# Two PSUM banks for B's broadcast and two, not three, for the ring of TensorE results

## The chip, the cores and the metric

The kernel runs on one core of one Trainium2 chip. The metric is the time of one execution on the device, in microseconds. It was run three times: the median is 8001.87 us, the lowest 7986.92, the highest 8004.43. Engines are called TensorE (PE in the profile, PEld its weight loads), VectorE (DVE), ScalarE (ACT), GpSimd (POOL) and SyncE (SP, which issues the DMAs).

## The reference

The input is 16 samples of 64 x 64 positions (tokens) with 96 channels. Two layers follow each other, each of them `x = x + layer(groupnorm(x))`, in 32 groups of three channels.

```python
# layer 0: a pointwise block between band-limited resamplings
xu = upsample_rfft(gn(x))                 # 64x64 -> 128x128
h  = xu @ W1.T + b1                       # 96 -> 384
h  = c0 + c1 * h + c2 * h * h
h  = h @ W2.T + b2                        # 384 -> 96
x  = x + lowpass_rfft(h)[::2, ::2]
# layer 1: Mamba over the 4096 tokens of a sample
xs, z = split(gn(x) @ W_in.T)             # 192 channels each
xc = silu(conv3(xs) + conv_b)
dt, B, C = split(xc @ W_x.T)              # 6, 16, 16
delta = softplus(dt @ W_dt.T + b_dt)
h_t = exp(delta_t * A) * h_{t-1} + delta_t * B_t * xc_t    # 192 x 16 states
y_t = sum_n(h_t * C_t) + xc_t * D
x  = x + (y * silu(z)) @ W_out.T
```

## The kernel before, in words

Each engine has one list of instructions, written out in the program's order, and semaphores between them. Layer 1 of sample s is what the loop runs on. The other work, of the samples behind it, is threaded in between: the S steps (transposes and the first half of the upsampling) of sample s + 2, the W steps (second half, W1, square, W2, first half of the low pass) and the D steps (second half of the low pass, residual) of sample s + 1.

A sample has 8 chunks (`NC8`) of 512 tokens. A chunk has 24 units (`NU`), and a unit is one scan: 32 channels x 4 states on 128 partitions, 512 tokens. Three units make a group, so there are 8 groups (`NG`) a chunk. For each group

- TensorE broadcasts the rows of B to 128 partitions in PSUM: `spread_b`, one bf16 matmul with `selb` into `pb` (L744),
- VectorE multiplies it with `rep_u` for three units at once into `b3`, in PSUM (L1021),
- VectorE does three scans `hs <- av, b3` (L1027), each of which needs its exponential `av` from ScalarE (L882; there are 8 buffers, so ScalarE can be 8 units ahead),
- GpSimd multiplies each with C into `hc` (L1068), and
- TensorE sums them over the states into `py` (`reduce`, L755; L752 adds the skip term at each half chunk). VectorE gates `py` (L1035), once at unit 15 and once at unit 3 of the chunk behind.

In TensorE's list the `spread_b` of group g + 1 stands at unit 3g + 1, and the `reduce` of group g at unit 3g + 5. `spread_b` waits until VectorE has done the product that read `pb` last, that of group g.

All other results of TensorE go through `cb`, a ring of PSUM banks, in steps: a step is one name in a plan (`plan_of`), and step i writes bank i modulo `RING`. It has to wait until the step that had the bank before was read (`freed_all([i - RING] + ...)`, L619). Most steps are read ("evicted") by ScalarE (L825, L832, L841, L856, L861, L867, L872), OUT at L800; SG, DG, WG and PAD by VectorE. The names are:

- W_up (two matmuls of L663, read at L825), W_f (L669, read with a square at L832), W_2 (twelve of L674, L825), W_dn (L680, L825),
- ST (L634), SA and SB (L639), D_lo and D_hi (L692 and L696; they wait for their loads `rr`, which SyncE issues as steps finish),
- the batch of a chunk, which stands in units 8 to 11 of TensorE's list: X, X (L708), Z, Z (L714), DBC (L718), DT, DT (L723) for the chunk two ahead,
- OUT (L735 and L736) at unit 6, and PAD (L622), which does nothing but bring a plan to a multiple of `RING`.

A plan has rows; a row is the unit at which a step stands in TensorE's list. W steps are spread evenly over the free rows of a sample (none stands in units 8 to 11 of a chunk). The other engines do their part of a step some units later in their own lists: `LAG` is 6 for ScalarE, 3 for VectorE, 2 for GpSimd, 1 for SyncE. The batch is evicted by ScalarE in one go at unit 14, with a table load ahead of the first silu, one ahead of the softplus, and one ahead of the next exponential, that of unit 15.

A full sample's plan has 273 steps. Ahead of the first sample lie 291 more with no scans beside them. The last sample has only batches and OUT.

Of the kernel before, what the change touches and what calls it, by code (L numbers as in the profile page):

```python
# [9 lines left out]
ALU = mybir.AluOpType  # L10
ACT = mybir.ActivationFunctionType

NS, HH, WW, C = 16, 64, 64, 96
# [8 lines left out]
T = 512  # L22
NC8 = L // T
NJ, NQ = DI // 32, DSTATE // 4
NU = NJ * NQ
NG = NU // 3
NHC, NAV, NHS = 6, 8, 6
XB_H = 8
LEAD = 2
RING = 3  # L30

# [20 lines left out]
def w_steps():  # L54
    out = []
    for b in range(NB + 3):
        if b < NB:
            out += [("W_up", b, r) for r in range(2)]
        if 1 <= b <= NB:
            out += [("W_f", b - 1, f) for f in range(NF)]  # L60
        if b >= 3 and (b % 2 == 0 or b == NB + 2):
            out.append(("W_dn", (b - 3) // 2))
        if 2 <= b <= NB + 1:
            out.append(("W_2", b - 2))
    return out
# [35 lines left out]
def padded(rows):  # L101
    rows = sorted(rows, key=lambda r: r[0])
    n = sum(st[0] not in UNRINGED for _, st in rows)
    return rows + [(rows[-1][0], ("PAD", i)) for i in range(-n % RING)]

# [30 lines left out]
def build(nc, A):  # L136
    ctx = ExitStack()
    with ctx:
        def sb(name, shape, dt=F32):
            return ctx.enter_context(nc.sbuf_tensor(name, shape, dt))  # L140

        def ps(name, shape):
            return ctx.enter_context(nc.psum_tensor(name, shape, F32))

        def sem(name):
            return ctx.enter_context(nc.semaphore(name))
# [15 lines left out]
        ident = sb("ident", [128, 128])  # L162
# [19 lines left out]
        selb = sb("selb", [C, NQ, 128], BF16)  # L182
# [17 lines left out]
        dm = sb("dm", [C, 2])  # L200
        spare = sb("spare", [C, RING])
        vv = sb("vv", [C, 2])
# [18 lines left out]
        bc3 = sb("bc3", [C, 4, T], BF16)  # L221
# [15 lines left out]

        cb = ps("cb", [128, RING, 512])
        b3 = ps("b3", [128, 3, 512])
        pb = ps("pb", [128, 512])  # L240
        py = ps("py", [128, 512])

        ld_w = sem("ld_w")
# [4 lines left out]
        pe_conv = sem("pe_conv")  # L248
        cb_free = [sem(f"cb_free{i}") for i in range(RING)]
        xb_ld = [sem("xb_ld0"), sem("xb_ld1")]  # L250
# [28 lines left out]
        pe_b = sem("pe_b")  # L279
        act_a = sem("act_a")  # L280
        dve_bu = sem("dve_bu")
# [35 lines left out]
        N_FREE = len(loads) - 2  # L317

        HEAD = w_steps()[:W_HEAD] + [("WLD", 0), ("WG", 0)]
        SETUP_STEPS = 3  # L320
        N_SETUP = 14
        BEFORE = [alone([("SLD", 0)] + s_steps() + [("SG1", 0), ("SG2", 0)]),
                  alone([("WLD", 0), ("WG", 0)] + w_steps(), [("SLD", 0)] + s_steps()),
# [4 lines left out]
        def ringed(plan):  # L328
            return sum(st[0] not in UNRINGED for _, st in plan)

        UF = ringed(FULL)
        starts = [SETUP_STEPS]
        for plan in BEFORE:
            starts.append(starts[-1] + ringed(plan))
        base_full = starts[-1]
        base_tail = base_full + LOOPS * UF
        assert ringed(FIRST) == UF and UF % RING == 0 and all(v % RING == 0 for v in starts)

        class Steps:
# [22 lines left out]
            def freed(self, i):  # L362
                return count(cb_free[i % RING], self.thirds + (i // RING + 1))

# [34 lines left out]
        def count(sm, v):  # L399

            return max(v, 0)
# [194 lines left out]
        def _(pe):  # L596
# [5 lines left out]
            for f in range(NF):  # L602
                mm = pe.matmul(cb[0:C, 1, 0:1], w2t[:, f, :], fcst[:, f:f + 1], start=(f == 0), stop=(f == NF - 1))
            mm.then_inc(pe_conv, 1)
            pe.transpose(cb[0:C, 2, 0:C], ident[0:C, 0:C], ident[0:C, 0:C]).then_inc(pe_conv, 1)
            pe.wait_ge(setup_v, count(setup_v, N_SETUP))
            pe.wait_ge(setup_a, count(setup_a, 2))

# [130 lines left out]
            def spread_b(G, k, g):  # L739

                if g == 0:
                    pe.wait_ge(pool_bc, count(pool_bc, G * 2 + 2))
                pe.wait_ge(dve_bu, count(dve_bu, G * NG + g))
                pe.matmul(pb[:, :], selb[:, g % NQ, :], bc3[:, k % 4, :], start=True, stop=True).then_inc(pe_b, 1)  # L744

            def reduce(s, k, g):
                G = s * NC8 + k
                hf, q = g // NQ, g % NQ
                pe.wait_ge(pool_hc, count(pool_hc, G * NU + 3 * g + 3))
                if q == 0:  # L750
                    pe.wait_ge(dve_y, count(dve_y, G * 2 + hf))
                    pe.matmul(py[0:C, :], ddiag[:, hf, :], xcs[:, k % 4, hf, :], start=True, stop=False,  # L752
                              skip_group_check=True)
                for j in range(3):
                    mm = pe.matmul(py[32 * j:32 * j + 32, :], rsel[:, :], hc[:, (3 * g + j) % NHC, :],  # L755
                                   start=False, stop=(q == NQ - 1), skip_group_check=True)
                mm.then_inc(pe_red, 1)

            def unit(s, k, n):
                G = s * NC8 + k  # L760
                if G == 0 and n == 0:
                    spread_b(G, k, 0)
                if n % 3 == AT["pe"]["pb"]:
                    if n // 3 + 1 < NG:
                        spread_b(G, k, n // 3 + 1)
                    elif not (G + 1 == NS * NC8):
                        spread_b(G + 1, k + 1, 0)
                if n % 3 == AT["pe"]["red"] % 3 and n >= AT["pe"]["red"]:
                    reduce(s, k, (n - AT["pe"]["red"]) // 3)

# [145 lines left out]
        def _(dve):  # L916
# [24 lines left out]
                setup(dve.tensor_scalar(ddiag[:, t, :], ident[0:C, 0:C], dskip[:, t:t + 1], None, ALU.mult))  # L941
            dve.wait_ge(setup_a, count(setup_a, 2))
            setup(dve.tensor_scalar(nega[:, :, :], nega[:, :, :], -1.0, None, ALU.mult))
            dve.wait_ge(pe_conv, count(pe_conv, 3))
            dve.tensor_copy(wlin[:, :], cb[0:C, 0, 0:C]).then_inc(cb_free[0], 1)
            dve.tensor_tensor(cbase[:, :], cb[0:C, 1, 0:1], b2t[:, :], ALU.add).then_inc(cb_free[1], 1)
            dve.tensor_copy(spare[:, 2:3], cb[0:C, 2, 0:1]).then_inc(cb_free[2], 1)
            assert n_set[0] == N_SETUP

            def step(st, key):  # L950
# [61 lines left out]
            def unit(s, k, n):  # L1012
                G = s * NC8 + k
                hf, g, q = n // 12, n // 3, n // 3 % NQ
                if n == 0:
                    dve.wait_ge(ru_ld[k % 2], count(ru_ld[k % 2], s * (4 * 64) + (k // 2 + 1) * 64))
                if n % 3 == 0:

                    dve.wait_ge(pe_b, count(pe_b, G * NG + g + 1))
                    dve.wait_ge(dve_h, count(dve_h, G * NU + n))  # L1020
                    dve.tensor_tensor(b3[:, :, :], rep_u[:, k % 2, 3 * hf:3 * hf + 3, :],  # L1021
                                      pb[:, None, :].broadcast_to([128, 3, T]), ALU.mult).then_inc(dve_bu, 1)
                    dve.wait_ge(pool_st, count(pool_st, G * NG + g + 1 - NHS // 3))
                    dve.wait_ge(dve_bu, count(dve_bu, G * NG + g + 1))
                dve.wait_ge(act_a, count(act_a, G * NU + n + 1))
                start = state[:, g, n % 3:n % 3 + 1] if k > 0 else zero_state[:, 0:1]
                dve.tensor_tensor_scan(hs[:, n % NHS, :], av[:, n % NAV, :], b3[:, n % 3, :], start, ALU.mult, ALU.add)\  # L1027
                    .then_inc(dve_h, 1)
                if n == AT["dve"]["y0"]:
                    gate(G, k, 0)  # L1030
# [141 lines left out]
```

## Time and profile before

| | |
|---|---|
| median of three runs | 8001.87 us |
| profiled execution | 7987.5 us |
| its span | 7985.7 us |
| granted TensorE clock, mean | 0.857 |
| TensorE busy | 6793.7 us, 85% |
| VectorE busy | 5981.0 us, 75% |
| ScalarE busy | 4697.4 us, 59% |
| GpSimd busy | 4578.7 us, 57% |
| L1021 `b`, x1024 | 1803.6 us busy, 1761 ns each |
| L1027 scans, x2688 and x384 | 3279.1 and 466.8 us busy, 1264 ns each |
| L744 broadcast, x1024 | 439.8 us busy, 429 ns each |

Busy is the time in which an engine ran an instruction, as a share of the span. The clock is the granted share of 2.4 GHz: 1.00 is the upper level and 0.50 the lower one, 1.2 GHz. An idle time is put down to the instruction that released the engine. In the rows below, a window's line has its start and end, its length, then each engine's busy time with the number of instructions, then the clock and the DMA engines' share and rate.

### The profile page before, as it was taken

The page shows a single profiled execution, that of the slowest core. Times are in us where ns is not written, and L with a number is a line of the kernel's source. Part 1 is how long each engine was busy: PE and PEld are TensorE (multiplying, and loading weights), DVE is VectorE, ACT ScalarE, POOL GpSimd, SP SyncE. Part 2 cuts the span into 40 slices and gives each one's busy share as a digit, 9 for nine tenths or more (in the row PEclk, how much of TensorE's full clock was granted, in tenths as well). Part 3 has the DMA queues.
Part 4 walks back from the last instruction along what each step waited for, and adds up shares of the span by engine and source line. Part 5 has one row for each costly group of instructions (what it writes and reads, how often), then busy time and mean ns, then how long its engine had stood idle before and what let it go on. Part 6 is the DMA issues. An engine that isn't in the chain of part 4 may idle for free. (4 is left out here: it accounts for less than half of the span.)

```text
span 7985.7 us, 102095 instructions
## 1 busy us (share of the span) xinstructions
PE 6793.7 (85%) x33686; PEld 3470.3 (43%) x33686; DVE 5981.0 (75%) x4943; ACT 4697.4 (59%) x8260; POOL 4578.7 (57%) x4516
## 2 busy tenths in 40 slices
PE   7897988979898897988979888897988979888666
PEld 5543444434344443444434444444443534444212
DVE  0287868778786886868778687787878878687788
ACT  4464756657475564756647566564755647566454
POOL 0265646656565564656656466565656656466566
PEclk8797988979798897988979889797998979889666
DMA  3455555545555554555555545555555655554542
GB/s 84 111 130 127 128 130 116 135 119 131 133 125 127 117 135 121 131 133 118 127 127 131 132 111 137 119 131 132 124 132 114 144 122 130 125 127 115 122 112 66
DMA packets 805834, 983.44 MB, mean 123 GB/s; under 512 B 391258, under 2 KB 417542, under 8 KB 805318
## 3 DMA queue, kind: packets, MB, share of 16 engines
q1 hardware_dynamic: 805318, 976.92, 51.8%
q8 instruction: 280, 4.59, 0.3%
q14 instruction: 236, 1.93, 0.1%
HBM read 717.71 MB, written 259.00 MB: 122 GB/s over the span
## 5 line engine op out<-in xcount | busy, mean ns | idle before, releaser
L1068 POOL TENSOR_TENSOR hc<-hs,cs 128x512 f32<-128x512 f32 x3072 | 3843.2, 1270 | 3022.5 <-DVE hs L1027 2005.9
L1027 DVE TENSOR_TENSOR_SCAN hs<-av,state,b 128x512 f32<-128x512 f32 x2688 | 3279.1, 1264 | 171.7 <-ACT av L882 97.2
L1021 DVE TENSOR_TENSOR b<-rep_u,pb 128x1536 f32<-128x1536 f32 x1024 | 1803.6, 1761 | 1215.3 <-PE pb L744 1152.7
L882 ACT ACTIVATE av<-rep_d,nega 128x512 f32<-128x512 f32 x3072 | 2124.8, 714 | 303.5 <-DVE hs L1027 299.6
L755 PE MATMUL py<-hc,rsel 128*32 128x512 f32 x6144 | 1292.4, 711 | 37.4 <-POOL hc L1068 36.6
L669 PE MATMUL cb<-xu,w1a 96*128 96x392 f32 x2400 | 1030.0, 540 | 86.3 <-ACT t1s L825 40.4
L674 PEld LDWEIGHTS cb<-w2c,g 128*98 128x98 f32 x9600 | 945.3, 177 | 193.2 <-issue 125.0
L674 PE MATMUL cb<-w2c,g 128*98 128x96 f32 x9600 | 973.2, 261 | 7.6 <-ACT g L832 6.6
L832 ACT ACTIVATE g<-cb,b1a 128x392 f32<-128x392 f32 x1200 | 686.3, 583 | 230.5 <-PE cb L669 215.2
L744 PE MATMUL pb<-bc,selb 96*128 96x512 bf16 x1024 | 439.8, 429 | 319.3 <-DVE b L1021 319.3
L708 PE MATMUL cb<-xn,wtap 96*96 96x512 f32 x1536 | 705.5, 609 | 1.1 <-ACT xn L904 1.1
L669 PEld LDWEIGHTS cb<-xu,w1a 96*128 96x128 f32 x2400 | 424.1, 198 | 558.6 <-issue 284.6
L841 ACT ACTIVATE x1s<-cb,cst 96x256 f32<-96x256 f32 x256 | 118.7, 470 | 644.4 <-PE cb L696 434.7
L663 PE MATMUL cb<-up_h,t1r 64*96 64x98 f32 x3200 | 386.1, 275 | 115.6 <-DVE b1a L999 60.4
L1027 DVE TENSOR_TENSOR_SCAN hs<-av,zero_state,b 128x512 f32<-128x512 f32 x384 | 466.8, 1264 | 14.3 <-ACT av L882 2.8
L692 PE MATMUL cb<-xt,wtot 96*96 96x256 f32 x512 | 240.8, 566 | 254.2 <-DMA rr<-v_scratch 158.0
L708 PEld LDWEIGHTS cb<-xn,wtap 96*96 96x96 f32 x1536 | 244.5, 166 | 475.2 <-issue 474.3
L755 PEld LDWEIGHTS py<-hc,rsel 128*32 128x32 f32 x6144 | 165.3, 115 | 633.3 <-issue 439.6
L663 PEld LDWEIGHTS cb<-up_h,t1r 64*96 64x96 f32 x3200 | 283.7, 169 | 350.2 <-issue 197.4
L825 ACT ACTIVATE vr<-cb 98x384 f32<-98x384 f32 x400 | 195.0, 488 | 407.5 <-PE cb L674 407.5
L856 ACT ACTIVATE xcs<-cb,tapb 96x512 f32<-96x512 f32 x256 | 175.0, 683 | 428.0 <-PE cb L708 428.0
L752 PE MATMUL py<-xcs,ddiag 96*96 96x512 f32 x512 | 328.4, 728 | 92.8 <-DVE xcs L1035 92.8
(102 smaller groups left out, 6762.8 us busy)
## 6 DMA issues: line engine op xcount, KB each, us to landing
rep_d<-delta_scratch SPq DMA_DIRECT2D x512, 384.0 KB, 7.2
rep_u<-deltax_scratch SPq DMA_DIRECT2D x512, 384.0 KB, 9.4
cs<-c_scratch SPq DMA_DIRECT2D x512, 256.0 KB, 5.6
delta_scratch<-dlt SPq DMA_DIRECT2D x128, 384.0 KB, 3.1
deltax_scratch<-dlt SPq DMA_DIRECT2D x128, 384.0 KB, 4.0
t_scratch<-t1s SPq DMA_DIRECT2D x128, 300.0 KB
t1r<-t_scratch SPq DMA_DIRECT2D x160, 240.0 KB, 5.0
rr<-v_scratch SPq DMA_DIRECT2D x256, 150.0 KB
```

The lines of the kernel that those rows point to most:

```text
L663: mm = pe.matmul(bank[0:C, e * GH:(e + 1) * GH], t1r[half, m % 2, i2 % 5, :], up_h[half, GH * r:GH * r + GH], start=True, stop=True)
L669: mm = pe.matmul(bank[:, 0:BC], w1a[:, 128 * f:128 * f + 128], xu[:, b % 2, :], start=True, stop=True)
L674: mm = pe.matmul(bank[0:GH, C * j:C * j + C], g2[:, b % 2, f, GH * j:GH * j + GH], w2c[:, f, :], start=(f == 0), stop=(f == NF - 1))
L708: mm = pe.matmul(bank[0:C, :], wtap[:, tap, t, :], xn[:, k2 % 2, tap:tap + T], start=(tap == 0), stop=(tap == 2))
L744: pe.matmul(pb[:, :], selb[:, g % NQ, :], bc3[:, k % 4, :], start=True, stop=True).then_inc(pe_b, 1)
L752: pe.matmul(py[0:C, :], ddiag[:, hf, :], xcs[:, k % 4, hf, :], start=True, stop=False, skip_group_check=True)
L755: mm = pe.matmul(py[32 * j:32 * j + 32, :], rsel[:, :], hc[:, (3 * g + j) % NHC, :], start=False, stop=(q == NQ - 1), skip_group_check=True)
L832: act.activation(g2[:, b % 2, f, :], bank[:, 0:BC], ACT.Square, bias=b1a[:, f:f + 1]).then_inc(fr, 1)
L882: act.activation(av[:, n % NAV, :], rep_d[:, k % 2, j, :], ACT.Exp, scale=nega[:, q, j:j + 1])\
L1021: dve.tensor_tensor(b3[:, :, :], rep_u[:, k % 2, 3 * hf:3 * hf + 3, :], pb[:, None, :].broadcast_to([128, 3, T]), ALU.mult).then_inc(dve_b ...
L1027: dve.tensor_tensor_scan(hs[:, n % NHS, :], av[:, n % NAV, :], b3[:, n % 3, :], start, ALU.mult, ALU.add)\
L1068: pool.tensor_tensor(hc[:, n % NHC, :], hs[:, n % NHS, :], cs[:, k % 2, g % NQ, :], ALU.mult)\
```

## The change

`pb` gets a second bank. The broadcasts run two groups ahead of the products, not one: at unit 3g + 1 TensorE writes the broadcast of group g + 2, into the bank that the product of group g has just read. The eight banks of PSUM were all in use (`cb` three, `b3` three, `pb` and `py` one each), so `cb` gives one up: `RING` is 2. With it go one transpose and one copy of the setup, and the plans are padded to even numbers of steps (274 for a full sample).

```diff
-RING = 3
+RING = 2
...
-        pb = ps("pb", [128, 512])
+        pb = ps("pb", [128, 2, 512])
...
-        SETUP_STEPS = 3
+        SETUP_STEPS = 2
...
-            pe.transpose(cb[0:C, 2, 0:C], ident[0:C, 0:C], ident[0:C, 0:C]).then_inc(pe_conv, 1)
...
-                pe.wait_ge(dve_bu, count(dve_bu, G * NG + g))
-                pe.matmul(pb[:, :], selb[:, g % NQ, :], bc3[:, k % 4, :], start=True, stop=True).then_inc(pe_b, 1)
+                pe.wait_ge(dve_bu, count(dve_bu, G * NG + g - 1))
+                pe.matmul(pb[:, g % 2, :], selb[:, g % NQ, :], bc3[:, k % 4, :], start=True, stop=True).then_inc(pe_b, 1)
...
                 if G == 0 and n == 0:
                     spread_b(G, k, 0)
+                    spread_b(G, k, 1)
                 if n % 3 == AT["pe"]["pb"]:
-                    if n // 3 + 1 < NG:
-                        spread_b(G, k, n // 3 + 1)
+
+                    if n // 3 + 2 < NG:
+                        spread_b(G, k, n // 3 + 2)
                     elif not (G + 1 == NS * NC8):
-                        spread_b(G + 1, k + 1, 0)
+                        spread_b(G + 1, k + 1, n // 3 + 2 - NG)
...
-            dve.wait_ge(pe_conv, count(pe_conv, 3))
+            dve.wait_ge(pe_conv, count(pe_conv, 2))
...
-            dve.tensor_copy(spare[:, 2:3], cb[0:C, 2, 0:1]).then_inc(cb_free[2], 1)
...
-                                      pb[:, None, :].broadcast_to([128, 3, T]), ALU.mult).then_inc(dve_bu, 1)
+                                      pb[:, g % 2, None, :].broadcast_to([128, 3, T]), ALU.mult).then_inc(dve_bu, 1)
```

## Rows read from the trace of the kernel before

**Rows 1.** The page: busy us, share of the span and instructions of each engine.

```profile
PE 6793.7 (85%) x33686; PEld 3470.3 (43%) x33686; DVE 5981.0 (75%) x4943; ACT 4697.4 (59%) x8260; POOL 4578.7 (57%) x4516
```

**Rows 2.** Waits, whole run: who waited for whom, us in total, times, longest.

```profile
DVE b L1021 <- PE pb L744: 1152.7, 396, 12.2
...
PE pb L744 <- DVE b L1021: 319.3, 113, 6.4
...
DVE hs L1027 <- ACT av L882: 100.0, 87, 1.7
```

**Rows 3.** Windows: chunks 0, 3, 5, 6 and 7 of one sample.

```profile
3731.52:3783.07 51.55, 47.05 (x269) 24.83 (x268) 44.33 (x35) 39.47 (x72) 33.45 (x35) 1.00 0.59 126
...
3893.44:3955.38 61.94, 57.48 (x305) 30.67 (x305) 45.55 (x37) 39.33 (x71) 36.43 (x37) 0.89 0.51 125
...
4019.31:4109.92 90.61, 65.32 (x270) 36.26 (x270) 53.88 (x51) 37.55 (x64) 32.88 (x32) 0.72 0.55 138
4109.92:4168.86 58.94, 45.10 (x155) 19.27 (x156) 49.62 (x45) 29.83 (x50) 36.80 (x38) 0.67 0.41 93
4168.86:4219.49 50.63, 48.43 (x269) 24.78 (x267) 44.26 (x34) 33.15 (x59) 35.92 (x37) 0.97 0.50 114
```

**Rows 4.** Waits of PE in 3731.5 to 4017, the first row of eleven.

```profile
PE cb L692 <- DMA xt<-xt_scratch: 6.0, 1, 6.0
```

**Rows 5.** Timeline of DVE in the last sample: start, us, what, idle before and releaser.

```profile
7648.11 1.76 DVE L1021 TENSOR_TENSOR b<-rep_u,pb 128x1536 f32<-128x1536 f32 x1 [1.95 <-PE pb L744]
...
7656.89 1.28 DVE L1027 TENSOR_TENSOR_SCAN hs<-av,state,b 128x512 f32<-128x512 f32 x1 [1.43 <-ACT av L882]
```

**Rows 6.** Timeline of ACT in the same stretch.

```profile
7656.04 4.40 ACT L882 ACTIVATE av<-rep_d,nega 128x512 f32<-128x512 f32 x7
```

**Rows 7.** Timeline of PE behind the batch of chunk 0.

```profile
3761.62 0.93 PE L669 MATMUL cb<-xu,w1a 96*128 96x392 f32 x2
3763.82 0.87 PE L680 MATMUL cb<-vr,dn_h 98*64 98x384 f32 x4 [1.27 <-ACT dlt L872]
...
3764.84 2.24 PE L674 MATMUL cb<-w2c,g 128*98 128x96 f32 x24
3767.01 1.06 PE L755 MATMUL py<-hc,rsel 128*32 128x512 f32 x6
3768.65 0.95 PE L663 MATMUL cb<-up_h,t1r 64*96 64x98 f32 x8 [0.58 <-ACT g L832]
3770.01 0.93 PE L669 MATMUL cb<-xu,w1a 96*128 96x392 f32 x2 [0.41 <-ACT vr L825]
```

**Rows 8.** Timeline of ACT in the same stretch.

```profile
3764.27 1.28 ACT L882 ACT_TABLE_LOAD   x1
3765.56 2.56 ACT L882 ACTIVATE av<-rep_d,nega 128x512 f32<-128x512 f32 x4
3768.03 0.57 ACT L832 ACTIVATE g<-cb,b1a 128x392 f32<-128x392 f32 x1
```

**Rows 9.** Timeline of PE behind the step WG in chunk 6.

```profile
4149.12 0.97 PE L663 MATMUL cb<-up_h,t1r 64*96 64x98 f32 x4
4154.63 0.96 PE L663 MATMUL cb<-up_h,t1r 64*96 64x98 f32 x4 [4.54 <-DVE b1a L999]
```

**Rows 10.** Groups of PE by line and shape: busy us, mean ns, idle before.

```profile
L622 PE MATMUL cb<-ident 96*96 96x96 f32 x9 | 2.8, 334 | 1.8 <-ACT dlt L872 1.8
```

**Rows 11.** Windows: chunk 0 of the sample before, and a stretch of chunk 3.

```profile
3246.34:3300.19 53.85, 51.15 (x282) 27.55 (x279) 44.36 (x34) 40.19 (x72) 35.36 (x36) 0.94 0.58 121
...
3930.00:3943.60 13.60, 10.57 (x35) 5.83 (x35) 8.66 (x7) 9.19 (x16) 5.37 (x8) 0.50 0.50 131
```

**Rows 12.** Waits in 4019.3:4219.5 (PE), 4109.9:4219.5 (DVE), 7570:7986 (DVE).

```profile
PE pb L744 <- DVE b L1021: 16.2, 5, 6.0
...
DVE b L1021 <- PE pb L744: 8.6, 6, 2.7
...
DVE b L1021 <- PE pb L744: 28.3, 11, 4.4
```

## The prediction

> **What bounds the kernel now.** I read the page first, then the waits, then one sample cut into its eight chunks, then timelines of single chunks. On the page the reader is to see TensorE busy 85% of the span and VectorE 75% [rows 1]. The list of waits shows what the change aims at: VectorE stood 1152.7 us before the product `b` (L1021) for TensorE's broadcast, TensorE 319.3 us before the broadcast for VectorE [rows 2]. If either were lost time, a second bank would be worth 4 to 14%. The third view says where it lies: in chunks 0 and 3 of the sample that starts at 3731.52, TensorE is busy 47.05 of 51.55 us and 57.48 of 61.94 (91 and 93%), VectorE only 44.33 and 45.55 [rows 3]. TensorE bounds chunks 0 to 4: of the eleven rows of waits it has in 3731.5 to 4017 none is for `b`. The largest is the one for a DMA [rows 4], most others are for ScalarE's evictions. Chunk 5 runs at DMA round trips and a clock of 0.72, chunk 6 at 0.67 with TensorE busy 45.10 of 58.94; chunk 7 has both engines nearly full, 48.43 and 44.26 of 50.63 [rows 3].
>
> **The second bank of `pb`.** It adds no instruction. `spread_b` stands at the same place of TensorE's queue and waits for the same product (g - 1 of two groups ahead is the g of one ahead), so nothing new is queued behind it; each broadcast is merely there one group earlier. In chunks 0 to 4 that saves VectorE waits where TensorE is the bound: worth 0. In chunks bounded by VectorE one has to ask what is late next. In the last sample `b` at 7648.11 waits 1.95 us for its broadcast; it would start at 7646.2. But two products later the scan of unit 15 at 7656.89 already waits 1.43 us for ScalarE [rows 5], whose exponentials restart at 7656.04 [rows 6], behind the evictions of the batch and three table loads, and those behind TensorE's batch of seven steps, which the second bank does not move. The saved 1.95 us becomes a wait of 3.4 us at the scan. The whole run has 87 such waits in 128 chunks, 100.0 us in all [rows 2], so I cost this part at 0 for each of them, and at -3 us once, in the last two chunks, which have no such batch. Bounds: 0, and all the waits that VectorE-bound places show, worked out below as a rival.
>
> **The ring of two banks.** Now step i waits until ScalarE has emptied the bank of step i - 2, not i - 3. ScalarE's order is fixed: it empties a step of row r after the exponential of unit r + 6. The dear place is behind the batch (X, X, Z, Z, DBC, DT, DT), and chunk 0 of the sample shows it. After the DTs TensorE does a W_f at 3761.62 (0.93), waits 1.27 us until 3763.82 for the first DT's eviction, does W_dn (0.87), W_2 at 3764.84 (2.24), the reduction (1.06), waits 0.58 us until 3768.65, does two W_up steps (0.95), and a W_f at 3770.01 [rows 7]. ScalarE evicts the DTs, loads a table from 3764.27 to 3765.55, does four exponentials from 3765.56, and only then evicts the first W_f, from 3768.03 to 3768.60 [rows 8]. With two banks that first W_f waits for the first DT's bank (free just before 3763.8, when W_dn started on it) and ends at 3764.7; W_dn ends at 3765.5; W_2 needs the bank of W_f, free at 3768.60, so it starts at 3768.65 instead of 3764.84, and the reduction ends at 3771.9. The W_up steps end at 3772.85, where the next W_f starts, not at 3770.01: **2.8 us later**. One chunk gives back 1.0 of the 3.8 us because TensorE stood still there before. Bounds for a batch: 0.9 us (one step such as the W_f put behind the wait) and 3.8 us (nothing given back). I take 2.8 for chunks 0 to 4: 14.0 us a sample.
>
> In chunk 6 the bank of WG is freed by VectorE at unit 160: W_up at 4149.12 (0.97) is done while waiting, and the next waits 4.54 us until 4154.63 [rows 9]. With two banks the first one waits too: 1.0 us. Chunk 7's batch I price at 1.1, by the lower bound, as VectorE shares the bound there. For short waits elsewhere (a step of 0.5 us between two evictions of about 0.5 us) I take 0.5 us in each of chunks 0 to 4, 2.5; bounds 0 and 8. The plan of a full sample has 273 steps; padded to an even number it gets one PAD more, a transpose of 0.33 us [rows 10] whose bank VectorE frees after its last scans: 1 us, bounds 0.3 and 4. Sum: 14.0 + 1.0 + 1.1 + 2.5 + 1.0 = 19.6 us a sample; low 7, high 33.
>
> **The clock.** Chunk 0 of the sample at 3246.34 took 53.85 us at a granted clock of 0.94 [rows 11], the same work a sample later 51.55 at 1.00 [rows 3]: 2.3 us for one short stretch at 1.2 GHz. In chunk 3 a longer one followed the waits behind the batch: 0.50, the lower level, in all of 3930.00 to 3943.60 [rows 11]. The ring adds idle time exactly there, so I add the small price in four more chunks: 9.2 us a sample; bounds 0 and half of 13.6 us in six chunks, 41. The Trainium skill, "TensorE: Matmul & The Clock Gate", section "A second HAM failure mode: psum-queue depth-cycling", says that cycling through PSUM banks can leave small idle gaps often enough for the clock to swing between its levels. It speaks against this change, and chunk 3 agrees; by it every batch would look like that one, which is my first rival.
>
> A second page bears on ScalarE's part: "ScalarE: Activation LUTs", section "What ACT_TABLE_LOAD costs", gives about 1.28 us for a load and 1.38 us of draining on top. The trace shows the 1.28 us, and the first exponential 0.01 us behind it [rows 8], so the 1.38 us is not charged here. By the page the bank of W_f would come that much later and each stall be 1.4 us longer, an estimate that the rows do not support.
>
> **The sum.** 14.3 samples' worth of such chunks (samples 0 to 13 whole, 14 in part; the last has no W steps): 14.3 x (19.6 + 9.2) = 412 us. The stretch ahead of the first sample uses the ring as well, with 291 steps and little beside them: +5. Setup loses one transpose and one copy: under 1 us, 0. Less 3 at the end: **+414 us**. The profiled execution took 7987.5 us (its span 7985.7), 14.4 under the median of 8001.87; I forecast against the median, rounded down a little since slowed matmuls give ScalarE time to catch up: **8400 us**, +5%.
>
> **Rivals.**
> 1. *Clock falls for long after each batch.* 19.6 + 41 = 61 us a sample, x 14.3 = 870, near 8870; halfway there 8650. For: chunk 3. Against: in other chunks waits of 2 to 3 us behind the batch cost a short stretch at most.
> 2. *The ring costs, but little.* PE's lateness is taken up where it waited anyway: in chunks 5 to 7 it has 16.2 us of waits for `b` [rows 12]. At the lower bounds, 7 us a sample less 2 for those: +70, 8070. Against: chunks 0 to 4 have no such waits.
> 3. *Faster.* The second bank pays where VectorE waits and TensorE has room: chunks 6 and 7 (8.6 us for broadcasts) and the last sample (28.3 us) [rows 12]: 15 x 8.6 + 28 = 157 us. It decides if the scan of unit 15 is not held by its exponential, and it wins from a ring cost under 11 us a sample; free of one: 7845. Against: rows 5 and 6.
> 4. *No change.* Both parts near nothing, or cancelling: 8002. The transfer of VectorE's wait from `b` to the scan makes this the likely outcome of the `pb` part alone, not of both.
>
> **How the numbers follow.** Forecast 0.60 (8120 to 8560 on its own), first rival 0.15, second 0.12, third 0.08, fourth 0.05. The range 8050 to 8650 leaves out the last two and the upper half of the first. A measurement of this kernel tells about 0.2% from no change: slower 0.60 + 0.15 + 0.12 = 0.87, same 0.05, faster 0.08.
>
> **What the profile after would show.** The wait of `b` for its broadcast falls from 1152.7 to under 300 us, and the scan's wait for `av` rises from about 100 to several hundred: right on the second bank. TensorE's waits for ScalarE's evictions rise by about 280 us, most at the third step behind each batch, about 3.8 us each: right on the ring. Mean clock falls from 0.857 to about 0.83. Chunk 0 takes about 57 us. I am wrong if chunks 0 to 4 keep their lengths, if chunk 7 or the last sample gets shorter by over 2 us a chunk, or if the third step behind the batch waits for something else.

## The result, and the profile after

The changed kernel takes 8396.9 us (median of four runs, 8391.13 to 8405.94) where the kernel before, on the same chip, takes 7999.7: 1.050 times as long, 95% interval 1.0482 to 1.0518. The forecast was 8400, the range 8050 to 8650.

First the page of the changed kernel, the line that answers to [rows 1] (its span is 8390.5 us):

```profile
PE 7078.9 (84%) x33694; PEld 3526.7 (42%) x33694; DVE 5986.0 (71%) x4951; ACT 4742.8 (57%) x8260; POOL 4569.9 (54%) x4516
```

VectorE, ScalarE and GpSimd do what they did before, within 46 us. TensorE has 8 matmuls more of 33,686 and is busy 285.2 us longer; it is idle 119.6 us longer. Together that is the whole of the 404.8 us by which the span grew. A busy time that grows with no work added is matmuls that take longer each: the clock is the first thing to ask about, and the mean granted clock fell from 0.857 to 0.844. It isn't the whole answer, as the part on the prediction shows.

Next the waits over the whole run, which answer to [rows 2]: who waited for whom, us in total, times, longest.

```profile
DVE hs L1027 <- ACT av L883: 781.5, 127, 7.3
DVE xcs L1035 <- PE py L754: 545.7, 154, 8.2
...
DVE b L1021 <- PE pb L743: 211.6, 79, 6.7
```

```profile
PE pb L743 <- DVE b L1021: 289.0, 92, 6.8
...
PE cb L668 <- ACT dlt L873: 95.3, 45, 2.2
...
PE cb L673 <- ACT g L833: 42.3, 48, 2.5
```

The wait that the second bank aims at fell by 941 us, and the kernel became slower. The wait one instruction further on, in front of the scan, which now waits for ScalarE's exponential, rose by 681.5 us, and that of the gate `xcs` for TensorE's sums rose from 164.0 to 545.7. The two rows for `cb` are new in this size: TensorE waits for the evictions of the step two back.

The windows of chunks 0, 3, 5, 6 and 7 of one sample answer to [rows 3]: start and end, length, then busy us and count of PE, PEld, DVE, ACT and POOL, the granted clock, the share of DMA and GB/s.

```profile
3944.96:4002.27 57.31, 49.69 (x269) 25.88 (x270) 44.38 (x35) 40.24 (x72) 32.89 (x33) 0.94 0.53 114
4119.99:4183.88 63.89, 57.87 (x299) 29.08 (x299) 45.67 (x37) 40.81 (x74) 36.62 (x36) 0.92 0.50 120
4243.14:4340.44 97.30, 72.17 (x291) 38.97 (x291) 53.94 (x51) 37.63 (x64) 37.22 (x37) 0.68 0.59 145
4340.44:4397.70 57.26, 43.12 (x145) 17.92 (x146) 49.62 (x44) 27.80 (x47) 36.49 (x38) 0.66 0.39 87
4397.70:4453.82 56.12, 53.04 (x279) 25.43 (x277) 44.49 (x36) 35.68 (x64) 38.25 (x38) 0.94 0.48 112
```

Chunk 0, with the same 269 matmuls as in [rows 3], went from 51.55 to 57.31 us: 2.6 us of it busy, 3.1 us idle.

One sample isn't enough, since chunks differ by 2 us from one to the next. The means over samples 1 to 13 (a chunk is counted from the start of its first product `b` to that of the next chunk; "ahead" is the stretch before the very first of them) show where the time went:

```
chunk        0    1    2    3    4    5    6    7   sum   | ahead  last sample
before     53.0 53.4 54.3 60.4 64.6 90.3 56.8 50.3  483.1 | 341.6  415.7
after      58.4 58.5 59.1 63.5 59.2 95.6 57.7 56.6  508.6 | 379.1  412.2
difference +5.4 +5.1 +4.8 +3.1 -5.4 +5.3 +0.9 +6.3  +25.5 | +37.5   -3.5
```

Behind the batch of chunk 0 the timeline of PE answers to [rows 7] (start, us, what, and in brackets the idle time ahead of it with its releaser). First the DTs of the kernel before, then the changed kernel:

```profile
3760.52 1.17 PE L723 MATMUL cb<-dbc,wdt 6*96 6x512 f32 x4 [0.21 <-ACT dbc L867]
```

```profile
3974.84 1.10 PE L722 MATMUL cb<-dbc,wdt 6*96 6x512 f32 x4 [0.21 <-ACT dbc L868]
3978.13 0.90 PE L668 MATMUL cb<-xu,w1a 96*128 96x392 f32 x2 [2.20 <-ACT dlt L873]
3978.96 1.11 PE L679 MATMUL cb<-vr,dn_h 98*64 98x384 f32 x4
3980.00 0.61 PE L743 MATMUL pb<-bc,selb 96*128 96x512 bf16 x1
3983.05 3.84 PE L673 MATMUL cb<-w2c,g 128*98 128x96 f32 x24 [2.44 <-ACT g L833]
3986.82 1.06 PE L754 MATMUL py<-hc,rsel 128*32 128x512 f32 x6
```

and that of ACT to [rows 8]:

```profile
3977.30 1.26 ACT L873 ACTIVATE dlt<-cb,bdt 96x512 f32<-96x512 f32 x2
3978.58 1.28 ACT L883 ACT_TABLE_LOAD   x1
3979.87 2.56 ACT L883 ACTIVATE av<-rep_d,nega 128x512 f32<-128x512 f32 x4
3982.34 0.57 ACT L833 ACTIVATE g<-cb,b1a 128x392 f32<-128x392 f32 x1
```

The reader is to see three things. The first step behind the DTs now waits for their eviction (2.20 us); before, it had a third bank and ran during it. The third, W_2 at 3983.05, waits until the first W_f is evicted, and that stands behind the table load and four exponentials on ScalarE. And W_2, released, takes 3.84 us for the 24 matmuls that took 2.24 in [rows 7]: the granted clock is 1.00 until 3979.4, 0.50 from 3979.5 to 3986.2 and 1.00 again after it. It fell behind the first wait, before the second had begun. From the start of the DTs to that of W_2 are 8.21 us; before, they were 4.32.

Last the place in the last sample that [rows 5] showed:

```profile
8065.22 1.28 DVE L1027 TENSOR_TENSOR_SCAN hs<-av,state,b 128x512 f32<-128x512 f32 x1 [3.34 <-ACT av L883]
```

The products run one group earlier and the scan waits 3.34 us; 3.4 was forecast.

### The profile page after: what moved, and what is told of

The parts are those of the page before. It is cut to its first block and busy times, and to the rows that moved or that the text cites. A ratio compares the mean times of both kernels' runs of the same rounds, so it can differ in the third digit from the quotient of the medians.

```text
span 8390.5 us, 101454 instructions
## 1 busy us (share of the span) xinstructions
PE 7078.9 (84%) x33694; PEld 3526.7 (42%) x33694; DVE 5986.0 (71%) x4951; ACT 4742.8 (57%) x8260; POOL 4569.9 (54%) x4516
## 5 line engine op out<-in xcount | busy, mean ns | idle before, releaser
L1027 DVE TENSOR_TENSOR_SCAN hs<-av,state,b 128x512 f32<-128x512 f32 x2688 | 3279.6, 1264 | 754.5 <-ACT av L883 682.6
L1021 DVE TENSOR_TENSOR b<-rep_u,pb 128x1536 f32<-128x1536 f32 x1024 | 1802.9, 1761 | 302.5 <-PE pb L743 211.6
L754 PE MATMUL py<-hc,rsel 128*32 128x512 f32 x6144 | 1310.6, 721 | 24.3 <-POOL hc L1068 24.3
L668 PE MATMUL cb<-xu,w1a 96*128 96x392 f32 x2400 | 1109.9, 566 | 137.6 <-ACT dlt L873 95.3
L673 PE MATMUL cb<-w2c,g 128*98 128x96 f32 x9600 | 1009.3, 267 | 111.1 <-ACT g L833 42.3
L743 PE MATMUL pb<-bc,selb 96*128 96x512 bf16 x1024 | 456.8, 446 | 289.0 <-DVE b L1021 289.0
L662 PE MATMUL cb<-up_h,t1r 64*96 64x98 f32 x3200 | 455.7, 285 | 140.8 <-DVE b1a L999 51.5
L1035 DVE TENSOR_TENSOR xcs<-zs,py 96x512 f32<-96x512 f32 x256 | 172.3, 673 | 545.7 <-PE py L754 545.7
L1027 DVE TENSOR_TENSOR_SCAN hs<-av,zero_state,b 128x512 f32<-128x512 f32 x384 | 466.8, 1264 | 109.4 <-ACT av L883 99.0
L662 PEld LDWEIGHTS cb<-up_h,t1r 64*96 64x96 f32 x3200 | 334.0, 177 | 401.5 <-issue 147.7
```

The costliest lines, as they stand in the source:

```text
L662: mm = pe.matmul(bank[0:C, e * GH:(e + 1) * GH], t1r[half, m % 2, i2 % 5, :], up_h[half, GH * r:GH * r + GH], start=True, stop=True)
L668: mm = pe.matmul(bank[:, 0:BC], w1a[:, 128 * f:128 * f + 128], xu[:, b % 2, :], start=True, stop=True)
L673: mm = pe.matmul(bank[0:GH, C * j:C * j + C], g2[:, b % 2, f, GH * j:GH * j + GH], w2c[:, f, :], start=(f == 0), stop=(f == NF - 1))
L743: pe.matmul(pb[:, g % 2, :], selb[:, g % NQ, :], bc3[:, k % 4, :], start=True, stop=True).then_inc(pe_b, 1)
```

## The experiments

In the diffs below the side marked + is the experiment; where nothing else is said it starts from the changed kernel.

### Which half costs: the ring alone

The ring of two banks can't be put on its own without one more edit: with one bank of `pb`, TensorE would wait in the unit of the step DG for a bank that VectorE frees only behind a product whose broadcast TensorE writes later in its list, and neither engine could go on. So the D steps start one unit later, and the first run measures that edit by itself, on the changed kernel.

```diff
-... even(d_steps(), 117, 132) ...
+... even(d_steps(), 118, 132) ...
```

> The changed kernel with one row moved: the D steps start at row 118, not 117. It is the control for the two kernels below, which need that. My theory (ring waits and the clock behind each batch make the +397 us) gives no change outside chunks 4 and 5: 8397 us within 20 us. A rival by which the place of the D steps against DG matters gives 10 to 40 us either way, all in chunks 4 and 5.

Measured 8390.8 us, ratio to the kernel before 1.0486 (1.047 to 1.0502): the same as the changed kernel. The edit is neutral, and the next run can be read against either.

```diff
-... even(d_steps(), 117, 132) ...
+... even(d_steps(), 118, 132) ...
...
-        pb = ps("pb", [128, 2, 512])
+        pb = ps("pb", [128, 512])
...
-                pe.wait_ge(dve_bu, count(dve_bu, G * NG + g - 1))
+                pe.wait_ge(dve_bu, count(dve_bu, G * NG + g))
...
-                    if n // 3 + 2 < NG:
-                        spread_b(G, k, n // 3 + 2)
+                    if n // 3 + 1 < NG:
+                        spread_b(G, k, n // 3 + 1)
...
```

> The ring of two banks alone: one bank of pb, one group ahead, as before; the D steps from row 118 (with 117 PE would wait in DG's unit for a bank that VectorE frees only after the next broadcast). My theory: the ring is the whole cost and the second bank of pb is worth about nothing, so 8397 us, within 1% of the control, at most 40 us above it where PE is late for a broadcast behind the batch. VectorE's wait of b for pb is back over 1200 us, the scan's wait for av back under 200. Rival 1: the second bank pays for part of the ring's cost, since PE is late by 2 to 4 us behind each batch and only a broadcast ready ahead hides it: 8500 or more, 3 to 6 us more per chunk. Rival 2: running two groups ahead is itself harmful: 8300 or less.

Measured 8426.9 us, 1.0529 (1.0512 to 1.0545). The ring alone costs 425 us against the kernel before on the same chip (8001.6), all of the change's loss and some more. The second bank, at a ring of two, is worth 36 us, 0.4%: the intervals of the two ratios, 1.047 to 1.0502 and 1.0512 to 1.0545, do not touch. Its waits on VectorE:

```profile
DVE b L1019 <- PE pb L743: 1502.2, 479, 10.6
DVE xcs L1033 <- PE py L754: 232.9, 98, 5.9
...
DVE hs L1025 <- ACT av L881: 34.8, 26, 1.6
```

1502.2 us of waits for the broadcast, and a second bank that takes away 86% of them is worth 36 us of time. Here, with the ring the same on both sides, one sees where they went: of the 1290.6 us, 746.7 come back in front of the scan (34.8 to 781.5) and 312.8 in front of the gate (232.9 to 545.7). Of the 36, 2 us are the last sample (414.5 against 412.2 us). The rest is spread: with two banks the mean sample is 2.8 us shorter (511.4 and 508.6; -2.1 in chunk 6, -1.7 in chunks 4 and 5 together, -1.4 in chunk 2, +2.1 in chunk 7), and the stretch ahead of the first sample 7 us longer.

### Whether the third step's wait is the loss: fewer exponentials in front of the eviction

ScalarE evicts the steps of row r behind the exponential of unit r + 6. At r + 3 one exponential, not four, stands between the table load and the eviction that TensorE waits for. The batch keeps its place.

```diff
-LAG = {"pe": 0, "act": 6, "dve": 3, "pool": 2, "sp": 1}
+LAG = {"pe": 0, "act": 3, "dve": 3, "pool": 2, "sp": 1}
```

> The changed kernel with ScalarE evicting a step of row r after the exponential of unit r + 3, not r + 6 (the batch stays at unit 14). Theory: the third step behind a batch waits for a bank whose eviction stands behind four exponentials; now it stands behind one, so the wait shrinks by about 1.9 us a batch, and the clock with it: 60 to 200 us faster than 8397. Rival: ScalarE now waits for PE with its exponentials unmade, so VectorE's scans wait for av instead, and the run is 0 to 200 us slower.

Measured 8241.9 us, 1.03 (1.0283 to 1.0318): 155 us of the 397 came back. The timelines of PE and ACT behind the same kind of batch:

```profile
3892.82 1.64 PE L668 MATMUL cb<-xu,w1a 96*128 96x392 f32 x2 [2.20 <-ACT dlt L873]
...
3896.28 3.34 PE L673 MATMUL cb<-w2c,g 128*98 128x96 f32 x24
```

```profile
3894.56 0.72 ACT L883 ACTIVATE av<-rep_d,nega 128x512 f32<-128x512 f32 x1
3895.19 0.57 ACT L833 ACTIVATE g<-cb,b1a 128x392 f32<-128x392 f32 x1
```

The first step waits the same 2.20 us, and W_2 waits no more: 3.46 us from the start of the first step to that of W_2, where the changed kernel has 4.92 and the kernel before 3.22 [rows 7]. W_2 is still slow, 3.34 us, though it waits for nothing: the clock is 1.00 until 3891.7 and 0.50 from 3891.8 to 3898.5. It fell during the first step's wait, which the shorter lag leaves as it was.

### What the clock is worth: work in the waits

The rival that gives the clock the larger share needs a run in which TensorE stays as late as it is and only its clock differs. I put matmuls that nobody reads into the two waits of the ring of two banks (one bank of `pb`, D steps at 118; the free bank takes their output). First trial: seven behind the second DT, ten at the third step.

```diff
+        du = ps("du", [128, 512])
...
+            since_dt = [9]
+            def fill(times):
+                for _ in range(times):
+                    pe.matmul(du[:, :], selb[:, 0, :], bc3[:, 0, :], start=True, stop=True)
...
+                    if key[0] == "DT" and key[2] == 1 and st.s >= 0:
+                        since_dt[0] = 0
+                        fill(7)
                     return
+                since_dt[0] += 1
+                if since_dt[0] == 3:
+                    fill(10)
```

> As e1_ring2_pb1 with matmuls that nobody reads, into the free eighth bank: 7 right behind the second DT and 10 ahead of the third step behind it, of 512 bf16 columns (about 0.22 us each at 2.4 GHz, 0.43 at 1.2), so that PE is busy in most of the two waits that the ring makes there. Theory: a good half of the cost is the clock, which falls after those waits. The mean clock of chunks 0 to 3 and 7 goes from about 0.92 to 0.96 or more, each loses 1.5 to 2.5 us, the run 100 to 200 us against e1. Rival: the waits alone cost, the clock would have fallen anyway; then no gain, or 0 to 60 us more because some fillers overrun the waits.

Measured 8719.6 us, 1.0894 (1.0876 to 1.0913), a miss. The timeline of PE says why:

```profile
4131.57 0.90 PE L681 MATMUL cb<-xu,w1a 96*128 96x392 f32 x2 [0.58 <-ACT dlt L884]
...
4136.49 4.42 PE L613 MATMUL du<-bc,selb 96*128 96x512 bf16 x10 [2.90 <-ACT g L844]
4140.71 1.53 PE L686 MATMUL cb<-w2c,g 128*98 128x96 f32 x8
```

The wait stands in front of the ten, not behind them: I had put them after the step's wait in the queue, and 4.42 us were paid in full on the path. The smaller version, four and four, has the same flaw:

> As d1_fill with 4 and 4 matmuls, not 7 and 10, so that they fit into the waits that e1_ring2_pb1 has there (2.1 us ahead of the first step behind the batch in every chunk, 0 to 2.8 ahead of the third). d1_fill brought the time at the lower clock from 2664 down to 2194 us, but its fillers took 642 us at the upper clock, more than the waits held. Theory: if idle time behind the batch is what lowers the clock, part of those 470 us comes back at under half the fillers' cost: 8427 down by 0 to 80 us. Rival: the clock needs all of the wait filled; then the fillers are paid in full, about 8 x 128 x 0.22 less the waits they fill, 8450 to 8550.

Measured 8551.6 us, 1.0695 (1.0675 to 1.0715). Neither answers the question. The third trial has seven behind the second DT again and puts the second group, four of them, ahead of the third step's wait:

```diff
                 if name not in BATCHED:
+                    since_dt[0] += 1
+                    if since_dt[0] == 3:
+                        fill(4)
...
+                    if key[0] == "DT" and key[2] == 1 and st.s >= 0:
+                        since_dt[0] = 0
+                        fill(7)
```

> Mends d1_fill and d2_fill_small, whose second group of fillers stood behind the third step's wait, not ahead of it, and so was paid in full. Here 7 fillers stand behind the second DT and 4 ahead of the wait of the third step behind it, else as e1_ring2_pb1 (8427 us). Theory: idle time behind the batch is what lowers the clock; the time at the lower clock falls by 300 us or more from 2664, the fillers cost little beyond the waits, and the run comes to 8300 to 8400. Rival: filling the waits doesn't help, because the clock falls in any case or the fillers overrun the short waits: 8430 to 8500.

Measured 8329.7 us, 1.0406 (1.0381 to 1.0431), 97 us faster than the same kernel without the 1358 extra matmuls of its trace (both read against the kernel before on their own chip, 1.0406 and 1.0529); granted clock 0.886, against 0.842 without them.

```profile
3932.23 1.10 PE L736 MATMUL cb<-dbc,wdt 6*96 6x512 f32 x4 [0.21 <-ACT dbc L880]
3933.26 1.69 PE L613 MATMUL du<-bc,selb 96*128 96x512 bf16 x7
3935.53 0.90 PE L682 MATMUL cb<-xu,w1a 96*128 96x392 f32 x2 [0.58 <-ACT dlt L885]
3936.36 0.87 PE L693 MATMUL cb<-vr,dn_h 98*64 98x384 f32 x4
...
3937.38 1.03 PE L613 MATMUL du<-bc,selb 96*128 96x512 bf16 x4
3940.45 3.83 PE L687 MATMUL cb<-w2c,g 128*98 128x96 f32 x24 [2.04 <-ACT g L845]
```

From the start of the DTs to the first step are 3.30 us, to W_2 8.22; the changed kernel has 3.29 and 8.21 (above). So here the extra matmuls cost no time, and what they give is clock: the time at the lower of its two levels falls from 2661 to 1891 us. The Trainium skill, "TensorE: Matmul & The Clock Gate", section "A second HAM failure mode: psum-queue depth-cycling", says that idle gaps from cycling through PSUM banks can pull the clock down; this run agrees in direction, with 97 us, 1.2%, for the idle time that it filled. That is not the ring's share: the 770 us at the lower level that it takes away are about twice the 376 that the ring alone had added (2284 to 2661), and 1891 is less than the kernel before has. The same matmuls in the kernel before were not tried. W_2 itself took 3.83 us even so: the idle 2.04 us in front of it were left, and the clock was 0.50 from 3941.0 to 3944.3.

### Whether a second bank pays where the ring keeps its three

The eight banks are full, so the pair can be had only if something else leaves PSUM. The buffer `b3` (three banks) went to SBUF; for room NAV went from 8 to 6 and ScalarE's lag from 6 to 4. On that base: ring three with one bank of `pb` and with two, then ring six with one and ring five with two. These start from the kernel before; the larger rings also have the transposes and copies of the setup that free their further banks.

```diff
-NHC, NAV, NHS = 6, 8, 6
+NHC, NAV, NHS = 6, 6, 6
-    "act": dict(xn=8, mid=23, batch=BATCH + 6),
+    "act": dict(xn=8, mid=23, batch=BATCH + 4),
-LAG = {"pe": 0, "act": 6, "dve": 3, "pool": 2, "sp": 1}
+LAG = {"pe": 0, "act": 4, "dve": 3, "pool": 2, "sp": 1}
+        b3 = sb("b3", [128, 3, T])
-        b3 = ps("b3", [128, 3, 512])
```

> A base with three PSUM banks to spare: the kernel before with the product b3 in SBUF, six buffers of av, not eight, to make room, and ScalarE's lag 4, not 6, to match (batch at unit 12). Ring of three, one bank of pb. If VectorE's product and scans take as long with b3 in SBUF and GpSimd isn't disturbed, 8000 us within 1.5%. Rival: fewer exponentials ahead cost VectorE 1 to 3 us a chunk: 8100 to 8400.

> n1_ring3_pb1 with the second bank of pb and two groups ahead; the ring keeps its three banks. My theory: the second bank alone is worth nothing, since the scan behind the batch waits for its exponential anyway and chunks 0 to 4 are bound by PE: the time of n1 within 0.3%. Rival: it takes away the 1152 us that VectorE waits and brings 100 to 160 us.

> n1_ring3_pb1 with six banks in the ring. Theory: the ring is what PE waits for in chunks 0 to 4 (about 3.3 us a chunk before) and a reason of the clock's dips, so 3 to 5 us a chunk in chunks 0 to 4, 200 to 350 us less than n1 and the fastest of all, about 7750. Rival: three banks were enough, PE's waits move to the next thing (hc, xcs): under 80 us.

> n1_ring3_pb1 with five banks in the ring and two of pb. Theory: within 0.3% of n3, since the fifth and sixth bank and the second of pb all do little. Rival: with the ring out of the way PE has room, and the second bank of pb pays at last: 50 to 150 us less than n3.

```
ring 3, one bank of pb    9238.2 us   1.1564 (1.1517 to 1.1612)
ring 3, two banks         9270.2 us   1.1581 (1.1558 to 1.1604)
ring 6, one bank          9200.2 us   1.1508 (1.1479 to 1.1537)
ring 5, two banks         9195.3 us   1.1500 (1.1481 to 1.1519)
```

The base is 16% slower than the kernel before, which I had not expected, and it is another kernel in what bounds it. The groups of the first, by line and shape (busy us, mean ns of one, idle before and what ended it):

```profile
L1027 DVE TENSOR_TENSOR_SCAN hs<-av,state,b 128x512 f32<-128x512 f32 x2688 | 4392.1, 1672 | 658.4 <-ACT av L882 576.1 <-DVE b L1021 1.3
```

```profile
L1068 POOL TENSOR_TENSOR hc<-hs,cs 128x512 f32<-128x512 f32 x3072 | 5551.4, 1826 | 1800.4 <-DVE hs L1027 1281.0 <-PE py L755 452.1 <-issue 47.7
L1072 POOL COPY state<-hs 128x3 f32<-128x3 f32 x1024 | 872.8, 852 | 0.0
```

Before, the same scan takes 1264 ns, GpSimd's product 1270 and its copy of the state 188. VectorE is the busiest engine at 80%. Even here, with three banks in the ring and VectorE the bound, the second bank brings nothing that can be measured (intervals 1.1517 to 1.1612 and 1.1558 to 1.1604). VectorE's 523.9 us of waits for the broadcast are gone with it, and its waits in front of the scan grew from 652.6 to 999.4 us. That speaks for the transfer of the wait, not for a loss hidden by the ring. A larger ring is worth 38 us with one bank of `pb` (six for three, and the intervals overlap) and 75 us with two (five for three, 1.1558 to 1.1604 and 1.1481 to 1.1519, which do not). On this base TensorE isn't the bound, so it doesn't tell what a fourth bank would bring to the kernel before. That stays open, and so does a second bank of `pb` beside three of the ring with `b3` in PSUM, which eight banks don't hold.

### The kernel before, with ScalarE's evictions earlier

If the wait behind the exponentials costs at two banks, the kernel before should have a little of it too.

```diff
-LAG = {"pe": 0, "act": 6, "dve": 3, "pool": 2, "sp": 1}
+LAG = {"pe": 0, "act": 3, "dve": 3, "pool": 2, "sp": 1}
```

> The kernel before (ring of three, one bank of pb) with ScalarE evicting a step of row r after the exponential of unit r + 3, not r + 6. With a ring of two that took 155 us off (8397 to 8242) by emptying the third step's bank behind each batch. Theory: with three banks the same wait stands one step later (1.27 to 2.8 us a batch before), so 20 to 80 us come off here: 7920 to 7980, the fastest so far. Rival: the one bank of pb and fewer exponentials made ahead cost VectorE more than that: 8010 to 8150.

> As l2_before_lag3 with 4 in place of 3. Theory: between the kernel before and that one: 7950 to 7990. Rival: nothing or slower, 8000 to 8080.

Lag 3 takes 7832.0 us, 0.9791 (0.9774 to 0.9809): faster than both kernels, and the fastest of all runs. Lag 4 takes 7884.3, 0.986 (0.9836 to 0.9884). Behind the batch, PE of lag 3:

```profile
3687.08 0.93 PE L669 MATMUL cb<-xu,w1a 96*128 96x392 f32 x2
3689.28 0.87 PE L680 MATMUL cb<-vr,dn_h 98*64 98x384 f32 x4 [1.27 <-ACT dlt L872]
...
3690.30 2.24 PE L674 MATMUL cb<-w2c,g 128*98 128x96 f32 x24
3692.48 1.06 PE L755 MATMUL py<-hc,rsel 128*32 128x512 f32 x6
3693.47 0.59 PE L663 MATMUL cb<-up_h,t1r 64*96 64x98 f32 x8
3693.99 0.93 PE L669 MATMUL cb<-xu,w1a 96*128 96x392 f32 x2
```

The two short waits behind the reduction (0.58 and 0.41 in [rows 7]) are gone, the 1.27 for the DTs is the same, and the mean sample is 472.8 us where it was 483.1. With lag 3 on both sides the change still costs 410 us (8241.9 against 7832.0): a shorter lag gives both kernels about the same, 155 us to the changed one and 169 to the one before (8001.4 on this chip). So the shorter lag doesn't repair the ring; it is a gain of its own.

## Why the prediction was right, step by step

**What bounds the kernel** held: TensorE in chunks 0 to 4, and VectorE's 1152.7 us of waits were slack. The run with the ring alone shows it best: taking away 1291 of its 1502 us of such waits is worth 36.

**The second bank at nothing, -3 at the end.** Right in place: the scan waits 3.34 us where 3.4 was worked out, and the last sample is 3.5 us shorter. Not foreseen were the other 33 of the 36 us that it is worth over the whole run at a ring of two: inside the chunks its price is small, but not nothing. The third rival (7845, the bank pays in chunks 6 and 7 and in the last sample) is refuted: chunk 6 of the ring-only kernel takes 59.8 us and of the changed one 57.7, so something of it is there, but chunk 7 goes the other way (54.5 and 56.6).

**The first and third step behind the batch.** The mechanism is right, and where it was walked through its size is too; for the other chunks it was too large. Means over samples 1 to 13 of the waits ahead of these steps, chunks 0 to 7:

```
              0    1    2    3    4    5    6    7
after, 1st  2.20 2.08 2.20 2.11 2.08 2.11 1.75 2.08
after, 3rd  2.05 1.86 0.32 2.80 0.07 0.00 3.62 0.16
before,1st  0    0    0    0    0    0    0    0
before,2nd  1.27 1.46 0    1.22 0.91 0.54 1.15 0.96
```

In chunk 0 W_2 came 3.8 us later in the walk, and 3.89 later in the trace (8.21 us behind the DTs, not 4.32). But the sign named for the profile took this delay for the idle time ahead of the third step, which by the same walk is 3.15 us (3765.5 to 3768.65) and was 2.44; and the first step's wait of 2.2 us, which the walk has too, was not named. The wait of the third step is 2 to 2.8 us in chunks 0, 1 and 3 and next to nothing in 2, 4, 5 and 7, since what step comes third differs. The 3.62 us of chunk 6 are VectorE's freeing of WG's bank, not ScalarE's evictions; before, they stood one step later [rows 9]. PE's waits for ScalarE in samples 0 to 14 rose by 166 us (302 to 468), 136 of them for the bank of a DT, and over the whole run by 171, not by 280. That chunk 2 still grew by 4.8 us, with 0.32 us ahead of its third step, is luck as far as this step goes.

The prediction charged no time between a table load and the first exponential; the rows of the changed kernel have 0.01 us there as well.

**Busy time that isn't the clock.** Samples 0 to 14 together grew by 371 us: 112 of TensorE idle, 259 busy. The forecast had 280 us of waits and 132 of clock. Take the matmul records of these samples that lie wholly at the upper level, so that the clock plays no part: those that write `cb` add 120 us more to TensorE's busy time than as many of the same kind did before, those that write `pb` and `py` 5 us less. With the ring alone it is 119 us more, with the ring of two at lag 3 it is 122, and with three banks at lag 3 it is 7 less. A pair of rows shows it, the four matmuls of Z in the batch of chunk 0, before and after, both at a granted clock of 1.00:

```profile
3755.51 1.88 PE L714 MATMUL cb<-xn,winz 96*96 96x512 f32 x4
```

```profile
3969.66 2.04 PE L713 MATMUL cb<-xn,winz 96*96 96x512 f32 x4
```

So the ring's cost stands in part as busy time. That a matmul which waits a little for its bank shows as a longer one fits: over the run the weight loads of Z now wait 97.2 us, 127 times, for ScalarE's evictions, and before never. This reading is argued; that the ring makes these 120 us is shown by the runs named.

**The clock.** Forecast 9.2 us a sample, 132 in all. The time at the lower level rose from 2284 to 2612 us in the run, and by 380 us in samples 0 to 14; if every matmul in it would run twice as fast at the upper level, that is worth 190 us at most, 13.3 a sample. What the idle 112 and the 120 us above leave of the 371 is 139 us, 9.7 a sample, near the forecast. But it is what is left over: no run gives back the ring's share of the clock alone, and the matmuls in the waits brought only 97 us for 770 at the lower level. Where the clock falls came out otherwise than priced. In chunks 0 to 4 and 7 of samples 1 to 13, 78 batches, it fell within 8 us behind the DTs 49 times in the kernel before and 78 times in the changed one; still 78 times with lag 3, where the third step waits for nothing in these chunks, and 38 times with the matmuls in the waits. That is 2.2 chunks a sample more, where four were priced, with longer stretches. So the first step's 2.1 us of standing still are enough for it; with those filled, it still falls behind the third step's wait in chunks 0 and 3 (13 and 12 times of 13). The first rival had the fall behind every batch right and its length wrong: the mean clock is 0.844, near the 0.83 that was expected, and its 8650 to 8870 us are refuted. Chunks 0 to 2, where the clock fell from 0.96, 0.97 and 0.98 to 0.92, 0.91 and 0.92, grew by 5.1 us on average; 2.8 + 0.5 + 9.2/5 = 5.1 were forecast.

**Where errors cancelled.** A sample grew by 25.5 us, 28.8 were forecast; all whole and part samples grew by 371 us, not 412. Chunks 4 and 5 together changed by -0.1 where some 5 us were forecast for chunk 4: one lost 5.4 and the other gained 5.3, and why, no run separated. Chunk 7 grew by 6.3, not 1.1 and a share of the clock: I priced it at the lower bound because VectorE shares its bound, and it doesn't, once TensorE is late (53.04 of 56.12 us busy in the window above, at a clock of 0.94 after 0.97). And the stretch ahead of the first sample, put at +5, grew by 37.5 us. That is the term that was mis-sized most. It is the ring too: 30.5 us of it with the ring alone, 0 with the kernel before at lag 3. The windows over it, before and after:

```profile
0.00:341.00 341.00, 275.44 (x1571) 183.96 (x1571) 27.67 (x79) 142.94 (x292) 11.13 (x13) 0.83 0.36 91
```

```profile
0.00:378.00 378.00, 309.58 (x1565) 196.28 (x1567) 27.23 (x75) 145.29 (x292) 11.12 (x13) 0.89 0.32 82
```

Here PE is busy 34 us longer for the same work at a higher granted clock, so this part isn't the clock. The same 64 matmuls of one step (L639 before, L638 after) take 26.8 us before and 34.4 after, with the shortest at 482 ns in both. It is the same lengthening of the ring's matmuls as in the samples, where steps follow each other without a gap.

So the sum was 414 and the measured 397 (404.8 between the two profiled spans): 371 in place of 412 from the samples, 37.5 in place of 5 ahead of them, -3.5 in place of -3 at the end.

## What to carry to other kernels

A second buffer for an operand pays only if the wait that it removes is the last one: before taking the bank, look at what the waiting engine's next instruction waits for. A ring's third bank is worth what stands between a result and its eviction on the evicting engine; behind a batch with a table load and a few operations of other work that was up to 2.8 us, and the clock's fall comes on top. Shorter waits for a bank can hide in the busy time: compare what the same matmuls take at the same clock. So before moving banks, try the cheap edit: take the eviction ahead of work that can wait, which here gave 2.1%.

## What the runs showed of the hardware

With `b3` in SBUF VectorE's scan went from 1264 to 1672 ns, GpSimd's product of 128x512 from 1270 to 1826 and its copy of 128x3 from 188 to 852: the scan had read one input from PSUM and now reads two from SBUF. The Trainium skill, "SBUF — State Buffer", section "Who interferes with whom", says that a VectorE instruction with two SBUF inputs contends with a GpSimd instruction that reads SBUF; these rows agree, for a scan as well, and put a size on it: 1.3 and 1.4 times as long, and 4.5 times for the small copy. VectorE's product `b`, which reads one input from SBUF and the other from PSUM in both kernels, kept its time (1761 and 1753 ns).

A short wait of TensorE costs more than it lasts. Behind the batch of chunk 0 the clock fell 1.3 us after the end of a wait of 2.20 us and stayed at the lower level for 6.8 us; in these W_2 took 3.84 us in place of 2.24, W_dn 1.11 in place of 0.87 and the broadcast 0.61 in place of 0.39. So 2.1 us of slower matmuls came on top of the two waits of 4.6 us.
